# Attention probabilities turned by VectorE and on-chip copies instead of TensorE

## What is computed

```python
w = codes * jnp.repeat(scales, 32, axis=0)           # for q, k, v, o
h = _layernorm(x) * (1 + ca) + sa                    # ca, sa, ... from silu(c) @ wmod
q, k, v = (h @ w_m + b_m for m in "qkv")             # heads of 128
attn = softmax(q @ k.T / sqrt(128))
x = x + ga * ((attn @ v) @ wo + bo)
h = _layernorm(x) * (1 + cb) + sb
x = x + gb * (h @ W.T + lora)                        # lora: top 2 of 8 experts of rank 16
```

## Time and profile before

| | us |
|---|---|
| runs of the kernel | 918.55, 919.41, 919.74; median 919.41 |
| span of the profiled execution (its own time beside it isn't given apart) | 918.8 |
| PE busy | 885.4 (96%), 4802 matmuls |
| DVE busy | 640.5 (70%) |
| ACT busy | 553.9 (60%) |
| POOL busy | 496.0 (54%) |
| DMA | 23.48 MB, mean 26 GB/s |

### The profile page before, as it was taken

One profiled execution on the slowest core, in us unless ns is written; L12 is line 12 of the kernel. 1 busy time (PEld: TensorE's weight loads), 2 busy tenths in 40 slices (PEclk: granted clock), 3 DMA queues, 4 the chain that ended last, 5 costly groups with the idle time before them and its releaser, 6 DMA issues.

```text
span 918.8 us, 15117 instructions
## 1 busy us (share of the span) xinstructions
PE 885.4 (96%) x4802; PEld 748.2 (81%) x4802; DVE 640.5 (70%) x1275; ACT 553.9 (60%) x1176; POOL 496.0 (54%) x497
## 2 busy tenths in 40 slices
PE   3899999999999999999999999999999999999878
PEld 2678888888888888888888888888888888887667
DVE  3678776776767666776767766677676767667884
ACT  2566766666666666666666666666666666665541
POOL 4554575457644575446654575546654575443341
PEclk9999999999999999999999999999999999999999
DMA  6200001000100011000100010000100001000002
GB/s 193 83 24 1 1 24 46 24 1 24 46 23 0 0 34 34 23 0 23 46 23 0 0 43 25 23 0 23 46 23 0 0 27 44 1 1 1 1 1 91
DMA packets 24657, 23.48 MB, mean 26 GB/s; under 512 B 3186, under 2 KB 24116, under 8 KB 24628
## 3 DMA queue, kind: packets, MB, share of 16 engines
q1 hardware_dynamic: 24628, 23.11, 8.1%
HBM read 21.01 MB, written 2.10 MB: 25 GB/s over the span
## 4 chain that ended last, share of the span: by engine, by line
PE 89%; DVE 5%; issue 1%; SPq 1%; ACT 1%; DMA 1%; POOL 0%; ACTq 0%; DVEq 0%; POOLq 0%
PE tr L1032 12%; PE qv L882 7%; PE qv L884 6%; PE qv L883 6%; PE score L882 6%; PE score L884 6%; PE score L883 6%; PE o L884 6%; PE o L882 6%; PE o L883 6%; PE ky L882 5%; PE ky L884 5%; PE ky L883 5%; PE y L882 2%; PE y L883 2%; PE y L884 2%
## 5 line engine op out<-in xcount | busy, mean ns | idle before, releaser
L348 POOL TENSOR_TENSOR prob<-prob,inv_sum 128x512 f32<-128x512 f32 x256 | 263.6, 1042 | 122.4 <-DVE inv_sum L720 122.4
L479 ACT ACTIVATE prob<-score,neg_max 128x512 f32<-128x512 f32 x256 | 176.4, 689 | 184.4 <-DVE neg_max L715 183.2
L715 DVE TENSOR_REDUCE neg_max<-score 128x1 f32<-128x512 f32 x256 | 177.0, 691 | 92.6 <-PE score L884 87.1
L724 DVE TENSOR_TENSOR pT_lo<-tr,pT_hi 128x512 fp32r<-128x512 f32 x256 | 174.7, 683 | 54.5 <-ACT pT_hi L493 54.4
L336 POOL TENSOR_TENSOR v_lo<-v,v_hi 128x512 fp32r<-128x512 f32 x64 | 82.6, 1291 | 237.2 <-ACT v L445 237.2
L493 ACT ACTIVATE pT_hi<-tr 128x512 fp32r<-128x512 f32 x256 | 152.2, 594 | 76.7 <-PE tr L1032 76.3
L1032 PE MATMUL tr<-ident,prob 128*128 128x128 f32 x1024 | 154.2, 273 | 2.6 <-DVE pT_lo L724 2.6
L1032 PEld LDWEIGHTS tr<-ident,prob 128*128 128x128 f32 x1024 | 124.4, 140 | 31.5 <-issue 4.2
L882 PE MATMUL score<-k_hi,q_hi 128*128 128x512 f32 x256 | 100.5, 392 | 1.3 <-ACT prob L479 1.3
L882 PE MATMUL o<-pT_hi,v_hi 128*128 128x512 f32 x256 | 99.8, 390 | 0.7 <-DVE pT_lo L724 0.7
L884 PE MATMUL o<-pT_hi,v_lo 128*128 128x512 f32 x256 | 100.1, 391 | 0.0
(11 more groups left out here) (227 smaller groups left out, 1805.8 us busy)
## 6 DMA issues: line engine op xcount, KB each, us to landing
stage<-in_L_attn_wq_codes_dram SPq DMA_DIRECT2D x8, 256.0 KB
stage<-in_L_attn_wq_scales_dram SPq DMA_DIRECT2D x16, 128.0 KB
stage<-in_L_attn_wk_codes_dram SPq DMA_DIRECT2D x8, 256.0 KB
stage<-in_L_attn_wk_scales_dram SPq DMA_DIRECT2D x16, 128.0 KB
stage<-in_L_attn_wv_codes_dram SPq DMA_DIRECT2D x8, 256.0 KB
stage<-in_L_attn_wv_scales_dram SPq DMA_DIRECT2D x16, 128.0 KB
stage<-in_L_attn_wo_codes_dram SPq DMA_DIRECT2D x8, 256.0 KB
stage<-in_L_attn_wo_scales_dram SPq DMA_DIRECT2D x16, 128.0 KB
```

The lines of the kernel that those rows point to most:

```text
L348: pool.tensor_tensor(prob[:, i], prob[:, i], inv_sum[:, i:i + 1].to_broadcast([P, S]), ALU.mult).then_inc(prob_ok, 1)
L479: act.activation(prob[:, i], score_ps[i % 2][:, :], ACT.Exp, bias=neg_max[:, i:i + 1], accum_out=row_sum[:, i:i + 1]).then_inc(exp_ok, 1)
L715: dve.tensor_reduce(neg_max[:, i:i + 1], score_ps[i % 2][:, :], AX.X, ALU.max, negate=True).then_inc(max_ok, 1)
L724: dve.tensor_tensor(pT_lo[:, s % 2, :, i * P:(i + 1) * P], tr_ps[i % 2][:, :].rearrange("p (k q) -> p k q", k=QT), pT_hi[:, s % 2, :, i * ...
```

## The change

**Transposition.** `transpose_probs` and the banks `tr_ps` go. DVE transposes `prob` in blocks of 32x32 (`turn`: one instruction for a tile of 128x512) into `pB`, in which the 32 rows of a block stay on the 32 partitions they came from. When all four tiles of a step are turned, SP issues 16 copies from SBUF to SBUF, of 32 partitions by 2 KB (64 KB), which bring every block to its partitions in `pT32`. `pB` and `pT32` are double, by the parity of the step. ACT makes `pT_hi` from `pT32`; the low part's four quarters (`kt`) are split: 0 and 1 by DVE, 2 and 3 by POOL, all from SBUF. `pT_hi` and `pT_lo` are single now.

**Order.** PV of step n-1 is done at the end of step n on PE, in one block, each `kt` behind its low part; the output projection of step n-2 in step n. The scores have four banks, o has two; the output projection writes into the score banks 2 and 3. V's half for the next step is projected a step later than before.

**Rest.** The stage of the weights has 8 places instead of 12 (the product overwrites the scales). SP's order is fixed in the step: the next pair's V and Q weights behind the 16 copies of step 0, K's behind step 1's, O's behind step 2's. In the last pair, the modulation (now computed in columns), the guard, the FFN weights and `gb` for all partitions move from the tail into steps 2 to 6, the gating of batches 0 and 1 to POOL in steps 4 and 6, `attended(0)` into step 63.

```diff
-        stage = sb("stage", [P, 12, 2 * PW])
+        stage = sb("stage", [P, 8, 2 * PW])
...
-        pT_hi = sb("pT_hi", [P, 2, QT, S], f32r)
-        pT_lo = sb("pT_lo", [P, 2, QT, S], f32r)
+        G = P // 32
+        pB = sb("pB", [P, 2, G, QT, QT, 32])
+        pT32 = sb("pT32", [P, 2, G, QT, QT, 32])
+        pT_hi = sb("pT_hi", [P, QT, S], f32r)
+        pT_lo = sb("pT_lo", [P, QT, S], f32r)
...
-        score_ps = [bank("score0"), bank("score1")]
-        tr_ps = [bank("tr0"), bank("tr1")]
-        qv_ps, ky_ps, o_ps, y_ps = bank("qv"), bank("ky"), bank("o"), bank("y")
+        score_ps = [bank(f"score{i}") for i in range(QT)]
+        qv_ps, ky_ps = bank("qv"), bank("ky")
+        o_ps = [bank("o_even"), bank("o_odd")]
+        y_ps = score_ps[2:4]
...
+        def turned(par, kt):
+            return pT32[:, par, :, :, kt, :].rearrange("p a i q -> p i a q")
+        def split(v, kt):
+            return v[:, kt].rearrange("p (i a q) -> p i a q", i=QT, a=G)
...
+                    sp.wait_ge(pB_ok, QT * (n + 1))
+                    for a in range(G):
+                        for g in range(G):
+                            sp.dma_start(pT32[32 * g:32 * (g + 1), par, a], pB[32 * a:32 * (a + 1), par, g]).then_inc(p_land[par], 16)
...
+                        for kt in (2, 3):
+                            pool.wait_ge(p_hi_ok, QT * (n - 1) + kt + 1)
+                            pool.tensor_tensor(split(pT_lo, kt), turned((s - 1) % 2, kt), split(pT_hi, kt).bitcast(f32),
+                                               ALU.subtract).then_inc(p_lo_b, 1)
...
+            def prob_high(n, par, round_):
+                act.wait_ge(p_land[par], round_)
+                for kt in range(QT):
+                    act.activation(split(pT_hi, kt), turned(par, kt), ACT.Copy).then_inc(p_hi_ok, 1)
...
+                    def turn(i):
+                        dve.wait_ge(prob_ok, QT * n + i + 1)
+                        if i == 0 and not early:
+                            dve.wait_ge(p_land[s % 2], landed(p, s - 2))
+                        dve.transpose(pB[:, s % 2, :, i].rearrange("p g k q -> p k g q"),
+                                      prob[:, i].rearrange("p (k g q) -> p k g q", k=QT, g=G)).then_inc(pB_ok, 1)
...
+            def weighted(n, vpar, j, par):
+                for kt in range(QT):
+                    pe.wait_ge((p_lo_a, p_lo_b)[kt // 2], 2 * n + kt % 2 + 1)
+                    cut = (slice(None), vpar, kt, slice(j * HD, (j + 1) * HD))
+                    ins = three(o_ps[par][:, :], (v_hi[cut], v_lo[cut]), (pT_hi[:, kt], pT_lo[:, kt]),
+                                kt == 0, kt == QT - 1)
+                ins.then_inc(o_mm, 1)
...
-                    transpose_probs(0)
...
-                    transpose_probs(3)
```

More of the change, by code:

```diff
@@ L273, in _, with next_weights @@
[L273 to L277, removed]
+            def next_weights(m, p):
+                sp.wait_ge(w_ok[m], (1 if m == "v" else 2) * p)
+                load_weights(m, p)
@@ L279, in _ @@
+            pair(0, first=True)
+            with sp.Fori(1, PAIRS - 1) as p:
+                pair(p)
+            pair(PAIRS - 1, last=True)
             for i in range(2 * B):
@@ L373, in _ @@
             pair(PAIRS - 1, last=True)
[L374 to L390, removed]
+            N = SPP * PAIRS
+            gate(2)
+            inverse_std(B)
+            inverse_std(B + 1)
+            for kt in (2, 3):
+                pool.wait_ge(p_hi_ok, QT * (N - 1) + kt + 1)
+                pool.tensor_tensor(split(pT_lo, kt), turned(1, kt), split(pT_hi, kt).bitcast(f32),
+                                   ALU.subtract).then_inc(p_lo_b, 1)
+            times_gb(0)
+            inverse_std(B + 2)
+            times_gb(1)
+            inverse_std(B + 3)
+            for b in range(2, B):
                 times_gb(b)
@@ L402, in _ @@
             act.wait_ge(c_tr, 1)
-            act.activation(c_exp[:, :], o_ps[:, 0:B * DC], ACT.Exp, scale=-1.0).then_inc(c_exped, 1)
+            act.activation(c_exp[:, :], o_ps[0][:, 0:B * DC], ACT.Exp, scale=-1.0).then_inc(c_exped, 1)
             def scale_codes(p):
@@ new lines, in pair @@
+                    if last and s == 5:
+                        act.wait_ge(ffn_tr, 2)
+                        act.activation(agT[:, :, :], ky_ps[:, 0:DC * (ER + EXP)].rearrange("p (c o) -> p c o", c=DC),
+                                       ACT.Copy).then_inc(ffn_ev, 1)
+                    if last and s == 6:
+                        act.wait_ge(ffn_tr, 3)
+                        act.activation(bT[:, :], ky_ps[:, 0:O], ACT.Copy).then_inc(ffn_ev, 1)
+                    if end:
+                        for i in range(2):
+                            act.wait_ge(gbb_mm, i + 1)
+                            act.activation(gb_row[:, 2 * i:2 * i + 2], (ky_ps, qv_ps)[i][:, :].rearrange("p (b d) -> p b d", b=2),
+                                           ACT.Copy).then_inc(gbb_ok, 1)
@@ L781, in _ @@
-            pair(0, first=True)
-            dve.wait_ge(y_zero, 1)
-            with dve.Fori(1, PAIRS - 1) as p:
-                pair(p)
-            pair(PAIRS - 1, last=True)
-            N = SPP * PAIRS
             def attended(b):
@@ L804, in _ @@
+            pair(0, first=True)
+            dve.wait_ge(y_zero, DC)
+            with dve.Fori(1, PAIRS - 1) as p:
+                pair(p)
+            pair(PAIRS - 1, last=True)
+            N = SPP * PAIRS
+            attended(1)
+            o_low(N - 1, 0, slice(FEAT // P - 2, FEAT // P - 1))
+            ffn_rows(0)
             for c in range(DC):
-                y_add(DC * (N - 2) + c + 1, B - 1, c, False)
-            ffn_rows(0)
-            attended(1)
-            o_low(N, slice(FEAT // P - 1, FEAT // P))
+                y_add(DC * (N - 2) + c + 1, B - 1, c, False, y_ps[c])
@@ new lines, in pair @@
+                        if last and s == 3:
+                            pe.wait_ge(mod_ok, 5)
+                        if last and 3 < s < 7:
+                            pe.wait_ge(ffn_ev, s - 3)
+                        project(ky_ps, "k", nxt % 2, batch_of(nxt)).then_inc(k_mm, 1)
+                    if start:
+                        pe.wait_ge(vec_ok, 2)
+                        transpose_input(1, o_ps)
+                    if not early:
+                        pe.wait_ge(o_ok, n - 1)
+                        if s == 2 or s == 3:
+                            pe.wait_ge(w_ok["o"], 2 * p + s - 1)
+                        for c in range(DC):
+                            pe.wait_ge(exp_ok, QT * n + c + 3)
+                            out_project(c, s % 2, y_ps[c])
```

652 lines of the change are left out of this document (310 added, 342 removed).

## The result

The changed kernel took **1009.16 us** (median of 4, 1007.04 to 1012.0) against 918.98 us (median of 4, 917.46 to 919.74) before: ratio 1.098, interval 1.095 to 1.101. It is slower by a tenth, where 854 us and "faster" were forecast. The profiled execution has a span of 1005.2 us, 86.4 more than the 918.8 of before.

The account below looks back on a forecast made before the run. PE was taken to bound the kernel at 12.8 us a step; the new step was 11.1 + 0.5 for the queue's loop and DVE-POOL wait, plus 0.2: 11.8. 918.8 - 62 x 1.0 - 3.5 + 0.6 gave 854 us, range 810 to 945.

Parts of the forecast that it names:

- PE's floor: PE's step without the sixteen transposes: 12.80 - 1.77 = 11.03 us, if nothing else binds.
- the turn: DVE's transpose of 128x512 in 32x32 blocks, four a step: 0.60 us in a row, 0.68 alone.
- The rival of the slow turn: A turn takes 1.29 us on DVE, its loop 13.5 us, the kernel 959 us; decides from 1.12 us; chance 0.08.
- the landing: Time for the last 64 KB copy of a step to arrive after its issue starts: 1.8 us.
- the issue: SP's 16 copies a step start 0.47 us apart, as its first loads did: 15 x 0.47 = 7.05 us.
- The loop itself: Loop over SP's queue: copies' issues, last landing, ACT's high part, DVE's low part, last turn, hand-overs: 11.1 us a step.
- The third rival: SP's train of copies binds: 0.63 us an issue, loop 13.5 us, kernel 959 us; decides from 0.586; chance 0.17.
- the meeting of DVE and POOL: DVE's low parts, now reading SBUF only, wait for POOL's instructions: 0.5 us on the first, up to 0.65 on the second.
- the second rival: POOL wins the meetings, DVE's second low part waits longer: 12.2 us a step, kernel 879 us; chance 0.13.
- Ends: -3.5: Start and tail outside the loop: -1.4 us from V's second half leaving the start, -2.1 in the tail.
- move into PE's new idle time: nothing: Modulation and FFN weights, moved into PE's idle time, cost nothing as long as a step isn't PE's.
- Signs that were named: Right: PE busy about 93%, issues 0.47 us apart, turns about 0.68, DVE's low parts 0.7 to 1.5; wrong: issues beyond 0.55.

## Why the prediction was wrong, point by point

**Right: PE's floor.** Taking 16 transposes from a step was put at 1.77 us, to 11.03. With the train split and all low parts on DVE, PE has 64% of the chain and a step takes 11.4 us in the mean, most of them 10.7 to 11.6. DVE is busy 97% there, so the floor itself isn't measured alone.

**Right: the turn.** 0.60 in a row and 0.68 alone were taken; it takes 0.70 (0.62 in a row). The rival of the slow turn (1.29) is out, and so is the estimate of 1.24 us that stood beside it.

**Right: the landing.** 1.8 us was taken; it is 2.0. The Trainium skill (DMA: Bandwidth & Descriptors, Anatomy of one DMA) states its fit for transfers that GpSimd issues; taken over to these, which SP issues, it is an estimate of 2.15 us for 64 KB, and the trace has 1.98.

**Wrong: the issue, and with it the sign.** The step that failed is "SP's first issues start 0.47 us apart (0.73 to 1.20); 15 x 0.47 = 7.05". The copies start 0.633 apart, 15 x 0.633 = 9.50. The loop itself was the right one: with the measured terms it gives 13.44, and the trace has 13.43. The price came from two loads from memory, and the text gave as the reason that "a copy here is as plain". The copies inside SBUF have a price of their own, the same for 1 KB and for 2 KB a partition. The third rival had the mechanism, the place and the size (0.63 us an issue, a loop of 13.5, deciding from 0.586), and was given 0.17. Its evidence, the scale loads at 0.63, was an accident: those are another kind of transfer with another length (up to 1.13 us in the rows above). The Trainium skill (DMA: Bandwidth & Descriptors, Issuing engines are not separate DMA queues) says that issuing on several engines saves only sequencer time, "which is usually small relative to the DMA itself". For one copy that is so here, 0.59 against 1.98 us. For sixteen in a row it isn't: 9.5 us of issuing stand before the last landing, and six copies moved to the other queue are worth 96 us.

**Wrong as placed, right as a mechanism: the meeting of DVE and POOL.** The forecast put 0.5 us on the first low part, which waits for POOL's scalings. In the longer step the scalings are over by then, and it takes 0.60 in the loop. The meeting falls on the second low part and POOL's first, off the path as long as the train binds. Once the train is gone, it is the next bound: the second rival had 12.2 us a step for it, and 12.03 were measured with half of the copies and with the split. The Trainium skill (SBUF — State Buffer, Who interferes with whom) has it that a DVE instruction with two SBUF inputs and a GpSimd one that reads SBUF exclude each other; the trace agrees, with 0.65 against 1.56 us for the same instruction 1.2 us apart.

**The sum.** A step was forecast at 11.8 us and took 13.8, over 63 distances some 126 us of the error. The rest, 26 us, is in the term **"Ends: -3.5"**: the first pair, the last pair and the tail lost more than the loop's pace explains. At the loop's 1.0 us a step the first pair would have lost 8.0 and the last 7.0; they lost 13.2 and 17.5, and the tail 9.7, of which the start gave back 2.0. So the ends cost +23 instead of -3.5, and this is more than half of the 50 us between 1009 and the third rival's 959; some 19 more are its loop price, 0.7 a step above before, which had left out the weights in SP's queue. The train isn't what makes the ends dear: with half of the copies, where it no longer binds, the first pair takes the same 123.0 us, the last pair's seven distances 96.3 against 84.2 at the loop's pace, and the end 81.7. Part of it can be read in the timeline of the last pair, where a second step of the prediction failed, the sentence that modulation and FFN weights "move into PE's new idle time: nothing". PE's timeline in the last pair of the changed kernel:

```profile
857.48 0.51 PE L933 MATMUL o_odd<-pT_hi,v_hi 128*128 128x512 f32 x1 [1.19 <-DVE pT_lo L749]
...
860.13 0.63 PE L934 MATMUL o_odd<-pT_lo,v_hi 128*128 128x512 f32 x1
860.56 0.63 PE L935 MATMUL o_odd<-pT_hi,v_lo 128*128 128x512 f32 x1
860.99 3.89 PE L1007 MATMUL ky<-c_silu,stage 128*128 128x4 f32 x32
864.73 0.61 PE L933 MATMUL score<-k_hi,q_hi 128*128 128x512 f32 x1
865.13 0.63 PE L934 MATMUL score<-k_lo,q_hi 128*128 128x512 f32 x1
```

PE is idle ahead of PV, since it waits for the low part; the modulation columns stand **behind** PV and ahead of the next scores, where all others wait for PE. They take 3.7 us in that step, which took 20.1 us; no run moved them, so what they cost the kernel is read and not shown. Idle time on an engine is no room for work that the program puts after the wait. The same rows show a second cost: matmuls 0.43 us apart, behind idle time, where they are 0.227 apart under load. That is a matmul at the lower of the two clock levels (1.2 instead of 2.4 GHz); the granted clock around them, and of the two tails (columns as rows 2: after twice, then before):

```profile
857.00:861.00 4.00, 3.52 (x10) 2.75 (x11) 2.28 (x4) 0.01 (x1) 2.80 (x2) 0.64 0.44 109
924.90:1005.20 80.30, 56.75 (x288) 46.83 (x286) 49.77 (x130) 22.55 (x52) 27.06 (x26) 0.89 0.15 45
```
```profile
848.20:918.80 70.60, 58.65 (x326) 48.09 (x324) 50.47 (x137) 24.76 (x57) 21.69 (x22) 0.98 0.09 30
```

Before, PE never idled in the loop and the granted clock was 1.00; here it is 0.92 in the first pair and 0.89 from the last first exponential on (0.98 in both before). In the tail PE is busy 56.75 us against 58.65 before, yet the tail is 9.7 us longer: what grew is its waiting, from 12.0 to 23.6 us. How the excess of the first pair divides between the clock, the batches' inputs on PE behind each wait and the late last turn wasn't separated.

**Signs that were named.** The text asked for issues 0.47 apart, and said that more than 0.55 would make it wrong. One line of the profile after decides it. PE's share of the span is 84% instead of about 93. Of the rest, ACT's wait for the copies, turns of 0.70 and DVE's low parts with a mean of 1.14 us came as described, in a kernel 155 us slower than forecast.

## What to carry to other kernels

When many small transfers on one queue stand in a loop, issue time times their number is a term of the loop like a matmul's, and it wants the price of that very kind of transfer: here 0.63 us inside SBUF against 0.47 from memory decided the sign, and the margin (it turned at 0.586) was thinner than the difference between the two kinds of row at hand. Look at what the first waiting instruction of an in-order engine holds back: a last turn behind one low part closed the loop, and one swap was worth 61 us. Work taken off the bound engine pays only if the replacements fit the loop's latency, not their engines' loads; when it does fit, count again what stands behind the new waits, at the lower clock.

## What the runs showed of the hardware

- A copy of 32 partitions of 2 KB inside SBUF keeps SP's sequencer for 0.59 us (0.633 from one to the next), and with 1 KB as well; the first of a train for 0.51. ACT's takes 0.61. Where the probabilities went through memory, their transfers of 0.25 and 1 MB took 0.30 to 0.43 us to issue.
- The two issuing engines do it side by side: 10 + 6 copies take the train out of the loop, and the landing stays at 2.0 us.
- A turn of 128x512 in 32x32 blocks of fp32 takes 0.70 us on DVE, about as much as a tensor_tensor of that size (0.68).
- One megabyte through memory and back in five transfers takes 3.9 + 1.3 + 6.2 us; sixteen copies inside SBUF take 9.5 + 2.0 for it.
- An instruction with two inputs in SBUF on each of DVE and POOL at once: DVE's goes from 0.65 to 1.56 us, POOL's from 1.29 to 1.5. With all low parts on DVE, its own stay at 0.68 and POOL's v_lo goes from 1.30 to 1.59; the kernel is 22 us faster than with half of them on POOL.
- Behind waits of 1.7 and 1.2 us in one step PE's matmuls ran 0.43 us apart instead of 0.227 for a while, and the granted clock of those 4 us was 0.64.
